# The two normalisations of the second norm stage: from VectorE to ScalarE, with a bias made by GpSimd

## The chip, the cores and the metric

The kernel runs on one core of one Trainium2 chip. The metric is the device time of one execution in microseconds (us), as the median of several runs. The engines of the core work side by side, each through its own list of instructions in order, and wait for one another on semaphores: TensorE (PE in the profile; its weight loads PEld), VectorE (DVE), ScalarE (ACT), GpSimd (POOL) and the DMA queues, of which SyncE (SP) issues most.

## The reference

The reference is two layers over 4096 tokens of 256 channels: `x = x + attention(norm(x)) + experts(norm(x))`, and then once more with other mixers. The part that matters here is where the second layer starts. It normalises each token, and one of its two mixers normalises the result again, with a weight and a bias of its own:

```
x  = x + L0_attn(xn, ...) + L0_ffn(xn, ...)
xn = _layernorm(x)                       # (x - m) / sqrt(v + eps)
x  = x + L1_attn(xn, ...) + L1_ffn(xn, ...)
# L1_ffn: mu, var of xn over the channels
#         z = (xn - mu) * rsqrt(var + EPS) * w + b, then q, k, v products of z
# L1_attn: q = elu(xn Wq + bq) + 1, k = elu(xn Wk + bk) + 1, v = xn Wv + bv, sums of k v
```

## The kernel before

The program is a row of phases with a barrier between them. The change lies in one, `phase_second_norm` (line 1382). It takes the 4096 tokens as 32 tiles of 128 tokens (on the partitions) by 256 channels, all in float32.

Each engine runs the same pipeline of steps (`steps`, line 1463). Step s works on four tiles at once: `a` is tile s, `b` tile s-1, `c` tile s-2 and `d` tile s-3. Four steps and the last five are written out, those between are a loop of two steps a pass. What each engine does in a step, in its own order, is the function `one` of its block:

- VectorE: `residual(a)` makes x1, the sum of the input, the attention result and two routed expert rows, and its statistics (L1716 to L1724); `sums(d)`; `keys_values(c)` (L1749 to L1753); `normed(a)` waits for the reciprocal root, makes xn1 (L1731, shown as `xn` in the profile) and the statistics of it (L1733, L1735); `queries(c)` (L1760, L1761, and L1763, which makes `k_feat`); `nested(a)` makes z (L1741); `values(c)` (L1769).
- GpSimd: `fetch(s + 1)`, two indirect DMAs that gather the routed rows of the next tile (L1531); `root(a, 0)`, which adds epsilon to the variance and raises it to -1/2 (L1540, L1542); `remainders(d)` (L1558, `qk_rest`); `root(a, 1)`, the same for the second norm; `add_base(a)` (L1547); `query_features(c)` (L1553).
- ScalarE: `key_exp(c)` (L1650); `low(d)` (L1681); `query_exp(c)` (L1654); `keep_turned(b)`, which takes the transposes of xn1 and z out of PSUM (L1660, and L1664 in two halves); `high(c)` (L1673, L1677).
- TensorE: `sums(d)` (L1627), which waits for `k_feat` of tile d; `linear(c)` (L1598, L1603); `nested_values(c)` (L1611); `turn(b)`, the transposes of xn1 and z (L1584, L1589); `nested_queries_keys(c)` (L1619).

So the order of each engine is written by hand, and `k_feat` of a step on VectorE (L1763), which stands behind the statistics of xn1, is what the next step on TensorE begins with.

Of the kernel before, what the change touches and what calls it, by code (L numbers as in the profile page):

```python
# [1381 lines left out]
def phase_second_norm(nc, g, ctx):  # L1382
# [4 lines left out]
    def sb(name, shape, dt=F32):  # L1387
        return ctx.enter_context(nc.sbuf_tensor(name, shape, dt))
# [13 lines left out]
    x1 = sb("x1", [P, 2, D])  # L1402
    stats = sb("s_stats", [P, 2, 2, 6])
    mean_var = sb("s_mean_var", [P, 2, 2, 2])
    var_eps = sb("s_var_eps", [P, 2, 2])
    rstd = sb("s_rstd", [P, 2, 2])
    xn1 = sb("xn1", [P, 2, D])
    base = sb("base", [P, 2, D])
    z = sb("z", [P, 2, D])
# [27 lines left out]
    cleared = sem("cleared")  # L1437
    x_d = [sem(f"x_in{r}") for r in range(2)]
    routed_in = [sem(f"routed_in{r}") for r in range(2)]
    half_d, routed_d, x1_d, st1_d, mv1_d, ve1_d, rs1_d, xn1_d, st2_d, mv2_d, ve2_d, rs2_d, z_d = (  # L1440
        sem(n) for n in ("half", "routed", "x1", "st1", "mv1", "ve1", "rs1", "xn1", "st2", "mv2", "ve2", "rs2", "z"))
    xnt_d, xns_d, zt_d, zs_d, kv_d, q_d, qk_d, v_d = (sem(n) for n in ("xnt", "xns", "zt", "zs", "kv", "q", "qk", "v"))
    kpre_d, vone_d, kmin_d, kexp_d, kf_d, sum_d, acc_d, qmin_d, qmax_d, qexp_d, qf_d = (
        sem(n) for n in ("kpre", "vone", "kmin", "kexp", "kf", "sum", "acc", "qmin", "qmax", "qexp", "qf"))
# [73 lines left out]
    @block.gpsimd  # L1518
    def _(pool):
        po = nc.gpsimd  # L1520
        po.memset(zeros[:], 0.0).then_inc(cleared, 1)
        po.memset(v_ones[:], 1.0).then_inc(cleared, 1)
        po.memset(g.v_one[:], 1.0).then_inc(cleared, 1)

        def fetch(t):

            r = t % 2
            if t >= 2:
                pool.wait_ge(x1_d, t - 1)
            for k in range(TOPK):  # L1530
                po.indirect_dma_start(share[:, r, k, :], None, g.y_d[:, :], bass.IndirectOffsetOnAxis(ap=g.slot[:, t, k:k + 1], axis=0)  # L1531
                                      ).then_inc(routed_in[r], 16)

        fetch(0)

        def root(a, n, mv_d, ve_d, rs_d, used_d):

            r = a.r
            wait_apart(pool, g, (used_d, a.free), (mv_d, a.t + 1))
            po.tensor_scalar(var_eps[:, r, n:n + 1], mean_var[:, r, n, 1:2], EPS, None, ALU.add).then_inc(ve_d, 1)  # L1540
            pool.wait_ge(ve_d, a.t + 1)
            po.tensor_tensor(rstd[:, r, n:n + 1], var_eps[:, r, n:n + 1], g.minus_half[:], ALU.pow).then_inc(rs_d, 1)  # L1542

        def add_base(a):
            pool.wait_ge(base_out[a.r], a.uses * 16)
            pool.wait_ge(xn1_d, a.t + 1)
            po.tensor_tensor(base[:, a.r, :], x1[:, a.r, :], xn1[:, a.r, :], ALU.add).then_inc(base_d, 1)  # L1547

        def query_features(c):
            pool.wait_ge(q_out[c.r], c.uses * 16)  # L1550
            pool.wait_ge(qmax_d, c.t * KC + KC)
            pool.wait_ge(qexp_d, c.t + 1)
            po.tensor_tensor(q_feat[:, c.r], q_max[:, c.r], q_min[:, c.r], ALU.add).then_inc(qf_d, 1)  # L1553

        def remainders(d):
            pool.wait_ge(lo_d, d.free)
            pool.wait_ge(hi_d, d.t + 1)
            po.tensor_tensor(qk_rest[:, d.r], qk_f[:, d.r], qk_parts[:, d.r, 0], ALU.subtract).then_inc(rest_d, 1)  # L1558

        for s in range(NT + 3):  # L1560
            a, c, d = (Tile(t, t % 2, t // 2) if 0 <= t < NT else None for t in (s, s - 2, s - 3))
            if s + 1 < NT:
                fetch(s + 1)
            if a is not None:
                root(a, 0, mv1_d, ve1_d, rs1_d, xn1_d)
            if d is not None:
                remainders(d)
            if a is not None:
                root(a, 1, mv2_d, ve2_d, rs2_d, z_d)
                add_base(a)  # L1570
            if c is not None:
                query_features(c)
# [71 lines left out]
    def _(act):  # L1644
        a_ = nc.scalar
# [6 lines left out]
        def query_exp(n):  # L1652
            act.wait_ge(qmin_d, n.t * KC + KC)
            a_.activation(q_min[:, n.r], q_min[:, n.r], ACT.Exp).then_inc(qexp_d, 1)  # L1654

        def keep_turned(b):
            t, r = b.t, b.r
            act.wait_ge(q_d, b.free)
            act.wait_ge(xnt_d, t + 1)
            a_.activation(xn1_t[:, r], p_xn[:, 0:D].rearrange("p (c t) -> p c t", c=KC), ACT.Copy).then_inc(xns_d, 1)  # L1660

            wait_apart(act, g, (qk_d, b.free), (zt_d, t + 1))
            for c in range(KC):
                last = a_.activation(z_t[:, r, c, :], p_z[:, c * P:(c + 1) * P], ACT.Identity,  # L1664
                                     bias=norm_t[:, 1, c, bass.ds(t, 1)], scale=norm_t[:, 0, c, bass.ds(t, 1)])
            last.then_inc(zs_d, 1)
# [12 lines left out]
        def low(d):  # L1679
            act.wait_ge(rest_d, d.t + 1)  # L1680
            a_.activation(qk_parts[:, d.r, 1], qk_rest[:, d.r], ACT.Copy).then_inc(lo_d, 1)  # L1681

        def one(ahead, a, b, c, d):
            if c is not None:
                key_exp(c)
            if d is not None:
                low(d)
            if c is not None:
                query_exp(c)
            if b is not None:  # L1690
                keep_turned(b)
            if c is not None:
                high(c)

# [3 lines left out]
    def _(dve):  # L1698
# [27 lines left out]
        def normed(a):  # L1726

            t, r = a.t, a.r
            dve.wait_ge(xnt_d, a.free)
            dve.wait_ge(rs1_d, t + 1)  # L1730
            v.tensor_scalar(xn1[:, r, :], x1[:, r, :], mean_var[:, r, 0, 0:1], rstd[:, r, 0:1], ALU.subtract, ALU.mult).then_inc(xn1_d, 1)  # L1731
            wait_apart(dve, g, (xn1_d, t + 1))
            v.bn_stats(stats[:, r, 1, :], xn1[:, r, :]).then_inc(st2_d, 1)  # L1733
            wait_apart(dve, g, (st2_d, t + 1))
            v.bn_aggr(mean_var[:, r, 1, :], stats[:, r, 1, :]).then_inc(mv2_d, 1)  # L1735

        def nested(a):
            t, r = a.t, a.r
            dve.wait_ge(zt_d, a.free)
            dve.wait_ge(rs2_d, t + 1)  # L1740
            v.tensor_scalar(z[:, r, :], xn1[:, r, :], mean_var[:, r, 1, 0:1], rstd[:, r, 1:2], ALU.subtract, ALU.mult).then_inc(z_d, 1)  # L1741

        def keys_values(n):

# [36 lines left out]
        def one(ahead, a, b, c, d):  # L1781
            if a is not None:
                residual(a)
            if d is not None:
                sums(d)
            if c is not None:
                keys_values(c)
            if a is not None:
                normed(a)
            if c is not None:  # L1790
                queries(c)
            if a is not None:
                nested(a)
            if c is not None:
                values(c)

        steps(dve, one)
# [585 lines left out]
```

## Time and profile before

| | us |
|---|---|
| median of 3 runs | 4898.24 (4896.6 to 4906.5) |
| the profiled execution: its time | 4895.71 |
| its span, first to last instruction | 4893.9 |
| its phase of the change: the first z tile starts at | 2634.4 |
| the last z tile starts at | 2891.0 |

The profile page gives busy time of the engines over the whole span (PE 92%, DVE 70%, ACT 39%, POOL 27%), which is a mean over phases with different limits. The phase of the change is some 270 us of the 4893.9, 5.5% of it. For what follows the span is cut: the list of instructions in order of time shows, for each, the start, the duration, the engine, the line of the kernel, and in brackets how long its engine had been idle before and what ended that. Times in the lists are counted from the start of the span.

### The profile page before, as it was taken

How to read it: one execution, taken by the hardware profiler on the slowest of the kernel's cores; microseconds unless marked ns; L12 is line 12 of the kernel's file. 1: busy time of each engine (PE TensorE's matmuls, PEld its weight loads, DVE VectorE, ACT ScalarE, POOL GpSimd, SP SyncE). 2: the span in 40 equal slices, each digit the busy share in tenths (PEclk: the TensorE clock that was granted, in tenths of full speed). 3: DMA queues.
4: the chain of work that ended last, by engine and by line, in shares of the span. 5: the costliest groups of instructions: out<-in, count | busy, mean ns of one | idle time of the engine just before them, and what ended most of it. 6: DMA issues, size and time to landing. Idle time of an engine off the chain costs nothing. (4 is left out here: it accounts for less than half of the span.)

```text
span 4893.9 us, 158526 instructions
## 1 busy us (share of the span) xinstructions
PE 4516.1 (92%) x65039; PEld 2896.2 (59%) x65039; DVE 3435.6 (70%) x5960; ACT 1910.9 (39%) x2645; POOL 1311.2 (27%) x1489
## 2 busy tenths in 40 slices
PE   6787859999999999999996879999999999999998
PEld 6333328999999999998664653444444444444443
DVE  4788975656565656555335978878787878787877
ACT  1566641111111111111143434656565656565654
POOL 1354444343434343433004772000000000000000
PEclk9999979999999999999998988999999999999999
DMA  3421231111111111110233441000000000000000
GB/s 109 139 98 56 103 130 52 55 55 55 53 56 53 56 52 58 47 63 26 74 121 105 109 118 35 4 17 4 17 4 17 4 17 6 17 9 13 9 13 9
DMA packets 201336, 249.92 MB, mean 51 GB/s; under 512 B 52864, under 2 KB 132864, under 8 KB 199968
## 3 DMA queue, kind: packets, MB, share of 16 engines
q1 hardware_dynamic: 180240, 209.39, 13.7%
q0 software_dynamic: 6144, 16.79, 1.1%
q10 hardware_dynamic: 14352, 14.55, 0.9%
q8 instruction: 522, 8.55, 0.7%
q14 instruction: 78, 0.64, 0.0%
HBM read 135.27 MB, written 105.38 MB: 49 GB/s over the span
## 5 line engine op out<-in xcount | busy, mean ns | idle before, releaser
L2169 DVE TENSOR_REDUCE part_max<-p_m 128x1 f32<-128x512 f32 x2118 | 1362.9, 685 | 377.7 <-PE p_m L2011 370.2
L2151 ACT ACTIVATE prob<-p_s 128x1024 f32<-128x1024 f32 x1024 | 1047.7, 1023 | 748.6 <-PE p_s L2075 746.5
L2030 PE MATMUL p_o<-prob,v_one 128*64 128x512 f32 x4096 | 1055.2, 592 | 3.9 <-ACT prob L2151 0.5
L2011 PE MATMUL p_m<-keys,queries 96*64 96x512 f16 x4236 | 661.9, 387 | 26.9 <-DMA keys<-parts_d 19.3
L2075 PE MATMUL p_s<-queries,keys 97*64 97x512 f16 x4096 | 619.6, 380 | 0.0
L2075 PEld LDWEIGHTS p_s<-queries,keys 97*64 97x64 f16 x4096 | 228.9, 109 | 597.7 <-issue 592.4
L1979 POOL TENSOR_TENSOR attn<-o_num,o_inv 32x512 f32<-32x512 f32 x64 | 81.0, 1266 | 1452.1 <-DVE o_inv L2188 1445.6
L546 PE MATMUL p_proj<-xn_t_all,proj_w_sb 128*128 (+1 forms) x768 | 390.0, 651 | 78.3 <-ACT raw L572 70.3
L2011 PEld LDWEIGHTS p_m<-keys,queries 96*64 96x64 f16 x4236 | 239.1, 108 | 309.1 <-DVE part_max L2169 56.3
L2030 PEld LDWEIGHTS p_o<-prob,v_one 128*64 128x64 f32 x4096 | 288.8, 136 | 162.1 <-issue 15.8
L805 PE MATMUL pd_pre<-inv,step 64*64 64x64 f32 x10240 | 372.0, 219 | 4.1 <-issue 2.7
L805 PEld LDWEIGHTS pd_pre<-inv,step 64*64 64x64 f32 x10240 | 339.5, 135 | 30.6 <-issue 29.7
L609 DVE SCALAR_TENSOR_TENSOR conv<-raw,conv_w_sb,conv 128x512 f32<-128x512 f32 x384 | 312.2, 813 | 56.8 <-POOL raw L633 45.3
L546 PEld LDWEIGHTS p_proj<-xn_t_all,proj_w_sb 128*128 128x128 f32 x768 | 155.6, 209 | 303.8 <-issue 178.3
L805 PE MATMUL pd_pre<-inv_low,upper 64*64 64x64 f32 x8192 | 302.4, 219 | 16.5 <-issue 15.5
L840 PE MATMUL pd_low<-step,inv 64*64 64x64 f32 x8192 | 297.7, 219 | 4.6 <-issue 3.8
L1040 DVE TENSOR_TENSOR step<-pd_pre,const 128x512 f32<-128x512 f32 x320 | 214.9, 687 | 118.4 <-PE pd_pre L805 116.5
L805 PEld LDWEIGHTS pd_pre<-inv_low,upper 64*64 64x64 f32 x8192 | 275.8, 135 | 24.8 <-issue 21.6
L840 PEld LDWEIGHTS pd_low<-step,inv 64*64 64x64 f32 x8192 | 274.1, 135 | 11.2 <-issue 10.3
L1044 DVE TENSOR_TENSOR inv_low<-low,pd_low 128x512 f32<-128x512 f32 x256 | 175.9, 687 | 125.1 <-PE pd_low L840 125.1
L1054 DVE TENSOR_TENSOR inv<-inv,pd_pre 128x512 f32<-128x512 f32 x256 | 175.9, 687 | 91.3 <-PE pd_pre L805 88.3
L1107 POOL TENSOR_TENSOR upper<-rel,beta 128x512 f32<-128x512 f32 x64 | 66.6, 1040 | 626.9 <-ACT rel L952 626.9
(246 smaller groups left out, 6832.7 us busy)
## 6 DMA issues: line engine op xcount, KB each, us to landing
k_d<-qkv SPq DMA_DIRECT2D x8, 2048.0 KB, 7.5
q_d<-qkv SPq DMA_DIRECT2D x8, 2048.0 KB, 12.3
v_d<-qkv SPq DMA_DIRECT2D x8, 2048.0 KB, 7.4
sums<-sums_d SPq DMA_DIRECT2D x128, 128.0 KB, 2.9
k_t<-k_d SPq DMA_DIRECT2D x64, 256.0 KB, 3.3
q_t<-q_d SPq DMA_DIRECT2D x64, 256.0 KB, 3.6
v_t<-v_d SPq DMA_DIRECT2D x64, 256.0 KB, 4.6
slots_d<-zero ACTq DMA_DIRECT2D x1, 10112.0 KB, 31.9
```

The source lines that it names most:

```text
L546: last = te.matmul(p_proj[j % RING][:], g.proj_w_sb[:, n, c, p * P:(p + 1) * P], g.xn_t[:, c, bass.ds(b * BLK, BLK)], start=c == 0, stop=c ...
L609: v.scalar_tensor_tensor(rows, cols, w, rows, ALU.mult, ALU.add).then_inc(conv_d, 1)
L805: last = te.matmul(out[hs, p, :], lhs(p, hs), rhs(p, hs), start=True, stop=True)
L840: last = te.matmul(p_low[x][hs, p, :], inv[x][hs, p, :], step[x][hs, p, :], start=k == 1 and p == 0, stop=k == NL - 1, skip_group_check=True)
L1040: v.tensor_tensor(step[x][:], p_pre[x][:], over_pairs(masks[:, k - 1, :]), ALU.mult).then_inc(step_d[x], 1)
L1044: v.tensor_tensor(inv_low[x][:], low_1[x][:], p_low[x][:], ALU.add).then_inc(lowc_d[x], 1)
L1054: v.tensor_tensor(inv[x][:] if k < NL else inv_fin[:, n.ring[x]], inv[x][:], p_pre[x][:], ALU.add).then_inc(up_d[x], 1)
L2011: last = te.matmul(p_m[k % 2][x * HALF:(x + 1) * HALF, :], queries[0:ROW, p, hh, at:at + HALF], keys[0:ROW, 2 * p + hh, kb * BLK:(kb + 1) ...
L2030: product = te.matmul(p_o[64 * hh:64 * hh + VW, :], g.v_one[:, j, p, hh:hh + 2, :].rearrange("p a d -> p (a d)"), prob[:, j % 2, hh, :], s ...
L2075: last = te.matmul(p_s[j % 2][x * HALF:(x + 1) * HALF, hh, :], keys[0:KR, 2 * p + hh, at:at + HALF], queries[0:KR, p, hh, :], start=True, ...
L2151: a.activation(prob[:, j % 2], p_s[j % 2][:], ACT.Exp, scale=SCORE_SCALE).then_inc(exp_d, 1)
L2169: v.tensor_reduce(part_max[:, hh * SUB + sub, kb:kb + 1], p_m[k % 2][:], AX.X, ALU.max).then_inc(red_d, 1)
```

## The change

The subtraction of the mean and the multiplication by the reciprocal root, `(x - m) * r`, becomes one ScalarE activation `x * r + (-m * r)`, with r as its scale and a new value, `shift` = -m * r, as its bias, both one number per partition. GpSimd makes `shift` behind each root, and waits for the root first. ScalarE gets `normed(a)` and `nested(a)`, and its order is changed: `keep_turned(b)`, which was fourth, is now first. VectorE keeps the statistics and waits for ScalarE where it waited for GpSimd.

```diff
         def root(a, n, mv_d, ve_d, rs_d, sh_d, used_d):
             r = a.r
             wait_apart(pool, g, (used_d, a.free), (mv_d, a.t + 1))
             po.tensor_scalar(var_eps[...], mean_var[:, r, n, 1:2], EPS, None, ALU.add).then_inc(ve_d, 1)
             pool.wait_ge(ve_d, a.t + 1)
             po.tensor_tensor(rstd[...], var_eps[...], g.minus_half[:], ALU.pow).then_inc(rs_d, 1)
+            pool.wait_ge(rs_d, a.t + 1)
+            po.tensor_scalar(shift[:, r, n:n + 1], mean_var[:, r, n, 0:1], rstd[:, r, n:n + 1], -1.0, ALU.mult, ALU.mult).then_inc(sh_d, 1)
...
     @block.scalar
+        def normed(a):
+            t, r = a.t, a.r
+            act.wait_ge(xnt_d, a.free)
+            act.wait_ge(base_d, a.free)
+            wait_apart(act, g, (sh1_d, t + 1))
+            a_.activation(xn1[:, r, :], x1[:, r, :], ACT.Identity, bias=shift[:, r, 0:1], scale=rstd[:, r, 0:1]).then_inc(xn1_d, 1)
+
+        def nested(a):
+            t, r = a.t, a.r
+            act.wait_ge(zt_d, a.free)
+            wait_apart(act, g, (sh2_d, t + 1))
+            a_.activation(z[:, r, :], xn1[:, r, :], ACT.Identity, bias=shift[:, r, 1:2], scale=rstd[:, r, 1:2]).then_inc(z_d, 1)
...
         def one(ahead, a, b, c, d):
+            if b is not None:
+                keep_turned(b)
+            if a is not None:
+                normed(a)
             if c is not None:
                 key_exp(c)
             if d is not None:
                 low(d)
+            if a is not None:
+                nested(a)
             if c is not None:
                 query_exp(c)
-            if b is not None:
-                keep_turned(b)
             if c is not None:
                 high(c)
...
     @block.vector
         def normed(a):
             t, r = a.t, a.r
-            dve.wait_ge(xnt_d, a.free)
-            dve.wait_ge(rs1_d, t + 1)
-            v.tensor_scalar(xn1[:, r, :], x1[:, r, :], mean_var[:, r, 0, 0:1], rstd[:, r, 0:1], ALU.subtract, ALU.mult).then_inc(xn1_d, 1)
             wait_apart(dve, g, (xn1_d, t + 1))
             v.bn_stats(stats[:, r, 1, :], xn1[:, r, :]).then_inc(st2_d, 1)
             wait_apart(dve, g, (st2_d, t + 1))
             v.bn_aggr(mean_var[:, r, 1, :], stats[:, r, 1, :]).then_inc(mv2_d, 1)
-
-        def nested(a):
-            t, r = a.t, a.r
-            dve.wait_ge(zt_d, a.free)
-            dve.wait_ge(rs2_d, t + 1)
-            v.tensor_scalar(z[:, r, :], xn1[:, r, :], mean_var[:, r, 1, 0:1], rstd[:, r, 1:2], ALU.subtract, ALU.mult).then_inc(z_d, 1)
```

One step of ScalarE behind the loop, before (`k_min` is L1650, `qk_rest` tile d, `ps_xn` and `ps_z` the transposes of tile b):

```order
L1650 ACTIVATE k_min<-k_min 128x256
L1681 ACTIVATE qk_parts<-qk_rest 128x512
L1654 ACTIVATE q_min<-q_min 128x256
L1660 ACTIVATE xn_t<-ps_xn 128x256
L1664 ACTIVATE z_t<-ps_z,norm_t 128x128 x2
L1673 ACTIVATE qk_f<-ps_qk,qk_b 128x128 x4
L1677 ACTIVATE qk_parts<-qk_f 128x512
```

The same step of ScalarE after:

```order
L1676 ACTIVATE xn_t<-ps_xn 128x256
L1680 ACTIVATE z_t<-ps_z,norm_t 128x128 x2
L1664 ACTIVATE xn<-x,s_shift,s_rstd 128x256
L1653 ACTIVATE k_min<-k_min 128x256
L1697 ACTIVATE qk_parts<-qk_rest 128x512
L1670 ACTIVATE z<-xn,s_shift,s_rstd 128x256
L1657 ACTIVATE q_min<-q_min 128x256
L1689 ACTIVATE qk_f<-ps_qk,qk_b 128x128 x4
L1693 ACTIVATE qk_parts<-qk_f 128x512
```

The new `xn` (L1664) stands behind the copies of both transposes, which come last but one in TensorE's step; `z` (L1670) stands ahead of the exponential of the queries.

One step of GpSimd, before, from the fetch on:

```order
L1531 DMA share_tile<-y_d,slot 128x256
L1531 DMA share_tile<-y_d,slot 128x256
L1540 TENSOR_SCALAR s_var_eps<-s_mean_var 128x1
L1542 TENSOR_TENSOR s_rstd<-s_var_eps,minus_half 128x1
L1558 TENSOR_TENSOR qk_rest<-qk_f,qk_parts 128x512
L1540 TENSOR_SCALAR s_var_eps<-s_mean_var 128x1
L1542 TENSOR_TENSOR s_rstd<-s_var_eps,minus_half 128x1
L1547 TENSOR_TENSOR base<-x,xn 128x256
L1553 TENSOR_TENSOR q_feat<-q_max,q_min 128x256
```

The same step of GpSimd after:

```order
L1532 DMA share_tile<-y_d,slot 128x256
L1532 DMA share_tile<-y_d,slot 128x256
L1541 TENSOR_SCALAR s_var_eps<-s_mean_var 128x1
L1543 TENSOR_TENSOR s_rstd<-s_var_eps,minus_half 128x1
L1545 TENSOR_SCALAR s_shift<-s_mean_var,s_rstd 128x1
L1561 TENSOR_TENSOR qk_rest<-qk_f,qk_parts 128x512
L1541 TENSOR_SCALAR s_var_eps<-s_mean_var 128x1
L1543 TENSOR_TENSOR s_rstd<-s_var_eps,minus_half 128x1
L1545 TENSOR_SCALAR s_shift<-s_mean_var,s_rstd 128x1
L1550 TENSOR_TENSOR base<-x,xn 128x256
L1556 TENSOR_TENSOR q_feat<-q_max,q_min 128x256
```

Two rows are new, one behind each root. VectorE's step loses L1731 and L1741 and is otherwise as before; TensorE's and SyncE's orders are unchanged.

## Rows read from the trace of the kernel before

**Rows 1.** Busy time by stretch: one step with 0.80 clock, one with 1.00, 28 steps together.
```profile
core 0: us, PE busy (x) PEld busy (x) DVE busy (x) ACT busy (x) POOL busy (x), PEclk, DMA share, GB/s
2673.16:2681.73 8.57, 8.07 (x41) 5.97 (x41) 7.59 (x20) 3.99 (x12) 6.42 (x10) 0.80 0.39 104
2681.73:2690.00 8.27, 6.38 (x41) 5.11 (x41) 7.57 (x20) 4.09 (x12) 6.44 (x10) 1.00 0.43 116
2656.56:2891.18 234.62, 198.92 (x1121) 152.46 (x1121) 212.64 (x533) 113.62 (x309) 178.58 (x251) 0.91 0.40 108
```

**Rows 2.** TensorE's wait in those 28 steps: us in total, times, longest.
```profile
PE ps_sum L1627 <- DVE k_feat L1763: 35.9, 29, 1.9
```

**Rows 3.** TensorE in order of time, two steps: start us, us, engine, line.
```profile
2664.89 0.68 PE L1627 MATMUL ps_sum<-v_ones,k_feat 128*128 128x129 f32 x4 [1.95 <-DVE k_feat L1763]
...
2669.10 0.38 PE L1589 MATMUL ps_z<-const,z 128*128 128x128 f32 x2
...
2673.16 1.09 PE L1627 MATMUL ps_sum<-v_ones,k_feat 128*128 128x129 f32 x4 [1.89 <-DVE k_feat L1763]
2674.04 3.20 PE L1598 MATMUL ps_kv<-kv_w,xn_t 128*128 128x512 f32 x4
...
2679.06 0.38 PE L1589 MATMUL ps_z<-const,z 128*128 128x128 f32 x2
```

**Rows 4.** All engines in order of time, the end of the second of these steps.
```profile
2673.57 0.77 POOL L1553 TENSOR_TENSOR q_feat<-q_max,q_min 128x256 f32<-128x256 f32 x1
...
2676.88 0.24 POOL L1540 TENSOR_SCALAR s_var_eps<-s_mean_var 128x1 f32<-128x1 f32 x1
...
2677.76 1.15 POOL L1558 TENSOR_TENSOR qk_rest<-qk_f,qk_parts 128x512 f32<-128x512 f32 x1
...
2678.06 1.01 DVE L1753 TENSOR_SCALAR k_min<-k_pre 128x256 f32<-128x256 f32 x1
...
2678.98 0.40 DVE L1731 TENSOR_SCALAR xn<-x,s_mean_var,s_rstd 128x256 f32<-128x256 f32 x1
...
2679.49 0.43 DVE L1733 BATCH_NORM_STATS2 s_stats<-xn 128x6 f32<-128x256 f32 x1
...
2680.39 0.22 POOL L1540 TENSOR_SCALAR s_var_eps<-s_mean_var 128x1 f32<-128x1 f32 x1 [1.48 <-DVE s_mean_var L1735]
...
2680.70 0.57 POOL L1542 TENSOR_TENSOR s_rstd<-s_var_eps,minus_half 128x1 f32<-128x1 f32 x1
...
2681.03 0.42 ACT L1654 ACTIVATE q_min<-q_min 128x256 f32<-128x256 f32 x1 [0.99 <-DVE q_min L1760]
...
2681.23 0.94 POOL L1547 TENSOR_TENSOR base<-x,xn 128x256 f32<-128x256 f32 x1
...
2681.50 0.83 DVE L1741 TENSOR_SCALAR z<-xn,s_mean_var,s_rstd 128x256 f32<-128x256 f32 x1
2681.61 0.80 ACT L1664 ACTIVATE z_t<-ps_z,norm_t 128x128 f32<-128x128 f32 x2
...
2681.73 0.68 PE L1627 MATMUL ps_sum<-v_ones,k_feat 128*128 128x129 f32 x4 [0.50 <-DVE k_feat L1763]
...
2682.30 0.63 ACT L1673 ACTIVATE qk_f<-ps_qk,qk_b 128x128 f32<-128x128 f32 x2
```

**Rows 5.** Groups by line over those 28 steps: count, busy us, mean ns, idle.
```profile
L1731 DVE TENSOR_SCALAR xn<-x,s_mean_var,s_rstd 128x256 f32<-128x256 f32 x28 | 26.9, 961 | 0.1
```

**Rows 6.** Groups by line and shape, ScalarE and GpSimd, whole span.
```profile
L1664 ACT ACTIVATE z_t<-ps_z,norm_t 128x128 f32<-128x128 f32 x64 | 25.6, 454 | 2.3 <-PE ps_z L1589 2.3
L1328 ACT ACTIVATE e_act_h<-e_bank 128x128 f32<-128x128 f32 x79 | 21.9, 277 | 65.0 <-PE e_bank L1288 65.0
L1961 POOL TENSOR_SCALAR nest_ob<-nest_o,const 128x32 f32<-128x32 f32 x4 | 1.4, 352 | 0.0
```

**Rows 7.** In order of time, the first tile: z's transpose and ScalarE's copy.
```profile
2635.32 0.66 PE L1589 MATMUL ps_z<-const,z 128*128 128x128 f32 x2 [2.06 <-DVE z L1741]
...
2636.10 0.81 ACT L1664 ACTIVATE z_t<-ps_z,norm_t 128x128 f32<-128x128 f32 x2 [2.35 <-PE ps_z L1589]
```

More of the change, by code:

```diff
@@ L1406, in phase_second_norm @@
     rstd = sb("s_rstd", [P, 2, 2])
+    shift = sb("s_shift", [P, 2, 2])
     xn1 = sb("xn1", [P, 2, D])
@@ L1439, in phase_second_norm @@
     routed_in = [sem(f"routed_in{r}") for r in range(2)]
-    half_d, routed_d, x1_d, st1_d, mv1_d, ve1_d, rs1_d, xn1_d, st2_d, mv2_d, ve2_d, rs2_d, z_d = (
-        sem(n) for n in ("half", "routed", "x1", "st1", "mv1", "ve1", "rs1", "xn1", "st2", "mv2", "ve2", "rs2", "z"))
+    half_d, routed_d, x1_d, st1_d, mv1_d, ve1_d, rs1_d, sh1_d, xn1_d, st2_d, mv2_d, ve2_d, rs2_d, sh2_d, z_d = (
+        sem(n) for n in ("half", "routed", "x1", "st1", "mv1", "ve1", "rs1", "sh1", "xn1", "st2", "mv2", "ve2", "rs2", "sh2", "z"))
     xnt_d, xns_d, zt_d, zs_d, kv_d, q_d, qk_d, v_d = (sem(n) for n in ("xnt", "xns", "zt", "zs", "kv", "q", "qk", "v"))
@@ L1534, in _, with root @@
         fetch(0)
-        def root(a, n, mv_d, ve_d, rs_d, used_d):
+        def root(a, n, mv_d, ve_d, rs_d, sh_d, used_d):
             r = a.r
@@ L1564, in _ @@
             if a is not None:
-                root(a, 0, mv1_d, ve1_d, rs1_d, xn1_d)
+                root(a, 0, mv1_d, ve1_d, rs1_d, sh1_d, xn1_d)
             if d is not None:
@@ L1568, in _ @@
             if a is not None:
-                root(a, 1, mv2_d, ve2_d, rs2_d, z_d)
+                root(a, 1, mv2_d, ve2_d, rs2_d, sh2_d, z_d)
                 add_base(a)
@@ L1791, in one @@
                 queries(c)
-            if a is not None:
-                nested(a)
-            if c is not None:
                 values(c)
```

## The prediction

> **What bounds the stage now.** I read the busy time by stretch first. From 2656.56 to 2891.18 us, 28 steps take 234.62 us, 8.38 each. TensorE is busy for 198.92 of them, VectorE for 212.64, GpSimd for 178.58, ScalarE for 113.62 [rows 1]. VectorE is the fullest engine. The waits say the same: TensorE waits 35.9 us in 29 pieces for VectorE's `k_feat` [rows 2], and the list in order of time shows GpSimd idle for 1.48 us before the second root [rows 4], while VectorE's group of xn has 0.1 us of idle before it in 28 steps [rows 5]. So a step lasts as long as VectorE's list of work.
>
> The list in order of time then shows two things that the sums hide.
>
> First, one VectorE instruction in each step is long. With `qk_rest` running on GpSimd from 2677.76 for 1.15 us, `k_min` takes 1.01 us and xn behind it 0.40; where `qk_rest` meets xn, xn is the long one, and its mean is 961 ns [rows 4, 5].
>
> Second, TensorE's clock. After an idle of 1.89 us before `ps_sum` (TensorE then waits for `k_feat`) the granted clock falls to its 1.2 GHz level: the step from 2673.16 has 0.80 on the mean, the next 1.00, and from `ps_sum` to the transpose of z it takes 5.90 us (2673.16 to 2679.06) where it took 4.21 (2664.89 to 2669.10), 1.69 more [rows 1, 3]. Of the 28 steps, 15 begin with an idle of 1.87 us or more, and in 12 of these `ps_kv` takes 2.84 us or more, as the 3.20 in [rows 3]; the other 13 begin with 0.51 us or less, as the 0.50 in [rows 4], and all 13 run at the full clock. Today this hardly costs: the step with the low clock lasts 8.57 us against 8.27 [rows 1], 0.30 of the 1.69. VectorE has other work meanwhile, and TensorE catches up by a short idle in the next step.
>
> **What is removed.** Per step, VectorE loses xn (0.96 mean) and z (0.83) [rows 4, 5]: 1.79 of its 7.6 busy us. If VectorE's list still set the step, that would be the gain.
>
> **What is added.** On ScalarE two activations of 128x256 with scale and bias per partition. No row has that form from SBUF. The exponential of the same size takes 0.42 [rows 4]; 128x128 takes 454 ns with both operands per partition and 277 with neither [rows 6], 0.18 more. I take 0.42 + 0.18 = 0.60; the bounds are 0.42 (operands free) and 0.80 (as the pair of `z_t`) [rows 4]. On GpSimd two instructions `shift` of one element. The nearest rows are `var_eps` at 0.22 [rows 4] and a `tensor_scalar` of 32 elements at 352 ns [rows 6]; I take 0.25. Each waits for its root, as the root waits for `var_eps`: 2680.39 + 0.22 to 2680.70, a gap of 0.09. So from root to the next instruction it takes 0.57 + 0.09 + 0.25 = 0.91 where it took 0.53 (2680.70 to 2681.23) [rows 4], 0.38 more, twice a step. GpSimd's idle hides that, if nothing waits for the root; now two things do.
>
> **What is moved, and closes a loop.** `keep_turned(b)` is now first on ScalarE, and xn of tile a stands behind it. So xn waits for TensorE's transposes, and these stand behind `ps_sum`, `ps_kv`, `ps_q`, `ps_v` of the same step. VectorE's statistics wait for xn, `queries` and `k_feat` stand behind the statistics, and the next step's `ps_sum` waits for `k_feat`. That is a ring, once round per step, in which nothing can run ahead. Before, xn waited for a root alone. I walk the ring with starts from [rows 3, 4, 7]:
>
> - statistics of xn to `ps_sum`: 2679.49 to 2681.73, 2.24;
> - `ps_sum` to the transpose of z: 4.21 at the full clock;
> - that transpose, 0.38 long, and the hop to ScalarE (2635.32 + 0.66 to 2636.10, 0.12): 0.50;
> - two copies `z_t` to the next ScalarE instruction: 2681.61 to 2682.30, 0.69;
> - xn 0.60 and the hop to the statistics (2678.98 + 0.40 to 2679.49, 0.11): 0.71.
>
> Sum 8.35 us at the full clock. In a step with the low clock all of the 1.69 lies on the ring: 10.04.
>
> A second ring runs through GpSimd, since ScalarE's `q_min` now stands behind z, and z behind `shift`: statistics to `var_eps` 0.90; to the root 0.31; to `shift` 0.66; `shift` and hop 0.37; z to the next activation 0.49 (0.60 less the overlap of 0.11 that the pair of `z_t` shows); exponential 0.42 and hop 0.11; that is 3.26 for `q_feat`. Then `q_feat` to the next step's `var_eps` 3.31 (2673.57 to 2676.88, with the two fetches between); root 0.31, `shift` 0.66, 0.37; xn and hop 0.71. Sum 8.62 [rows 4]. This sets the steps at the full clock. `base` is not late in it: 2.12 + 0.91 = 3.03 is before 3.26.
>
> Queued behind the waiting xn on ScalarE are `k_min`, `qk_parts` and z; they are awaited by `k_feat`, 1.68 us or more after the statistics, which leaves them time. The DMA of SyncE that follows `qk_parts` is not in a ring.
>
> **How often the clock falls.** After `ps_z` TensorE has `ps_qk` left. Round the first ring the idle before `ps_sum` is what it was in the steps that ended at 1.9, in every step, since TensorE no longer catches up: 0.50 is gone from the list. At the share of the trace, 12 of 15, that is 22 of 28 steps.
>
> The sum: 22 steps x (10.04 - 8.38) = 36.5; 6 x (8.62 - 8.38) = 1.4; for the filling and the end of the pipeline, where `shift` and a longer activation stand in the chain of each tile, 2, an estimate. Together +40 us. The profiled execution takes 4895.7 (span 4893.9), so 4936; the median shown is 2.5 above it: 4938. With activations of 0.42 it is 22 x 1.48 - 6 x 0.12 + 2 = +34, with 0.80 it is 22 x 1.86 + 6 x 0.64 + 2 = +47: 4932 to 4945.
>
> A rule on the clock, from the Trainium skill, "TensorE: Matmul & The Clock Gate", section "HAM oscillation — how this bites in real kernels", says that a loop which does a short burst of matmuls and then waits goes back to the half clock in every round. By the rule all 28 steps pay: 28 x 1.66 + 2 = +48, 4946; by the trace, 3 of 15 such idles were followed by no fall (one of them is the 1.95 before 2664.89 in [rows 3]), and the sum above goes by these.
>
> **Rivals.**
>
> *Faster: VectorE is relieved, and GpSimd becomes the bound.* For it: VectorE's and not TensorE's list is full, and the long xn goes. GpSimd would need 8.57 - 1.48 = 7.09 us and two times 0.38 more, 7.85: 28 x (7.85 - 8.38) = -15, 4883. It needs a first ring below 7.85, 0.50 less than the walk gives, and the low clock off it; if xn did not have to wait for the transposes it would be so. Against it stands the order of ScalarE, which puts them first. The skill's page "SBUF — State Buffer", section "Who interferes with whom", speaks for this rival: a VectorE `tensor_scalar` in its two-port mode and a GpSimd instruction lock each other out for the whole instruction, so taking two of them away frees both engines. The trace agrees on the cause (1.01 or 0.40 us for the same work, [rows 4]); but what it frees is time outside both rings.
>
> *Little change: the low clock stays hidden or grows rare.* If the falls hit `ps_qk`, which is in no ring, or came as seldom as one step in ten, the steps are at 8.62: 28 x 0.24 + 2 = +9, 4907. Against it: the falls came at once after the idle, in `ps_sum` or `ps_kv`, which are in the ring.
>
> *Half of the steps*, as 12 of 28 now: 14 x 1.66 + 14 x 0.24 + 2 = +29, 4927. For it: the fall has not come in two steps in a row in this trace. Against it: each was followed by a step with an idle of 0.51 or less, which the ring no longer gives.
>
> That the change does not do what it says can be left out: the order shows both activations and both shifts in each step.
>
> **Chances and range.** The forecast of +34 to +48 has 0.60, half of the steps 0.17, little change 0.10, faster 0.05, and 0.08 for more (hops of ScalarE longer than those of VectorE in both rings, 0.2 in each of 28 steps, 6 us more). The time is 4938. The range is 4905 to 4952; the likeliest case alone has 4928 to 4950. About 0.2% (9.8 us) is what a measurement of this kernel can tell from no change; the case of little change lies on that line. So slower 0.86, the same 0.09, faster 0.05.
>
> **What would show it.** In the profile after: steps of 10.0 us and of 8.6, no longer 8.57 and 8.27; VectorE idle before the statistics of xn (some 1.5 us at the full clock, 3 at the low one), released by ScalarE's xn; ScalarE's xn released by TensorE's `ps_z` in the steps with the low clock and by `shift` in the others; an idle of 1.9 to 2.1 us before every `ps_sum`, and no 0.5; a granted clock of 0.86 or so over the stage where it was 0.91; `k_min` still at 0.3 or 1.0. The prediction is wrong if the steps at the low clock are not longer by 1.4 or more, if they are less than half, or if xn starts before the transposes of its step.

## The result, and the profile after

The kernel after takes 4951.77 us (median of 4 runs, 4949.41 to 4954.13), the kernel before on the same chip 4901.93 (4 runs, 4896.6 to 4906.5). The ratio is 1.0102, with a 95% interval of 1.0085 to 1.012: slower by 49.8 us. Forecast were 4938, a range of 4905 to 4952, and slower with 0.86. The direction came out. The time lies at the upper edge of the range, 0.2 us inside it, and above the 4928 to 4950 of the likeliest case.

The profiled execution takes 4953.73 us (span 4951.9) where it took 4895.7 (span 4893.9). From the first z to the last z it is 305.7 us (2639.84 to 2945.56) against 256.5, so 49.2 of the 58.0 us of difference lie in the tile pipeline; 5.4 come up to the first z (4.0 of these ahead of the stage, in a part that the change does not touch) and 3.4 behind the last one, also untouched.

Busy time by stretch, kernel after: the stretch in us, its length, busy us (instructions) of the five engines, granted clock, DMA share, GB/s. A step at the low clock (one in which the granted clock falls to 1.2 GHz for a part of it), one at the full clock, and 28 steps together, against [rows 1].

```profile
core 0: us, PE busy (x) PEld busy (x) DVE busy (x) ACT busy (x) POOL busy (x), PEclk, DMA share, GB/s
2756.59:2766.75 10.16, 8.06 (x41) 6.02 (x41) 6.37 (x18) 5.06 (x13) 7.02 (x12) 0.83 0.34 92
2797.19:2806.21 9.02, 6.38 (x41) 5.11 (x41) 6.11 (x18) 5.28 (x13) 7.01 (x12) 1.00 0.35 96
2654.97:2937.10 282.13, 222.42 (x1120) 163.67 (x1121) 175.77 (x477) 141.87 (x364) 196.67 (x309) 0.84 0.34 90
```

A step lasts 10.08 us where it lasted 8.38. No engine is fuller than TensorE, with 7.9 of the 10.08 us, and part of that is the low clock's own doing. VectorE has fallen from 7.6 busy us per step to 6.3, as was wanted; GpSimd has 7.0. When no list of work fills a step, the order in which the engines wait for each other sets it.

Waits over these 28 steps, kernel after (who waits, for whom: us in total, times, longest), against [rows 2].

```profile
ACT xn_t L1676 <- PE ps_xn L1587: 90.9, 28, 3.4
DVE s_stats L1750 <- ACT xn L1664: 83.1, 28, 3.4
PE ps_sum L1630 <- DVE k_feat L1774: 62.2, 28, 4.5
POOL s_var_eps L1541 <- DVE s_mean_var L1752: 46.1, 28, 2.0
ACT z L1670 <- POOL s_shift L1545: 45.5, 28, 2.1
POOL q_feat L1556 <- ACT q_min L1657: 13.8, 28, 0.5
```

Read in a circle: ScalarE waits for TensorE's transposes, VectorE for ScalarE's xn, TensorE for VectorE's `k_feat`, each 28 times in 28 steps. Before, the third had 35.9 us [rows 2], and VectorE did not wait for xn at all [rows 5]. The last three rows are the second circle, through GpSimd.

The first circle in order of time, kernel after, one step at the low clock (start us, duration, engine, line, instruction; in brackets the idle before it and its releaser), against [rows 3, 4].

```profile
2754.35 0.43 DVE L1750 BATCH_NORM_STATS2 s_stats<-xn 128x6 f32<-128x256 f32 x1 [3.15 <-ACT xn L1664]
...
2756.59 0.68 PE L1630 MATMUL ps_sum<-v_ones,k_feat 128*128 128x129 f32 x4 [2.10 <-DVE k_feat L1774]
...
2757.11 2.99 PE L1601 MATMUL ps_kv<-kv_w,xn_t 128*128 128x512 f32 x4
...
2762.47 0.38 PE L1592 MATMUL ps_z<-const,z 128*128 128x128 f32 x2
...
2762.74 0.38 ACT L1676 ACTIVATE xn_t<-ps_xn 128x256 f32<-128x256 f32 x1 [3.39 <-PE ps_xn L1587]
...
2763.11 0.81 ACT L1680 ACTIVATE z_t<-ps_z,norm_t 128x128 f32<-128x128 f32 x2
...
2763.81 0.59 ACT L1664 ACTIVATE xn<-x,s_shift,s_rstd 128x256 f32<-128x256 f32 x1
...
2764.51 0.43 DVE L1750 BATCH_NORM_STATS2 s_stats<-xn 128x6 f32<-128x256 f32 x1 [3.15 <-ACT xn L1664]
```

From statistics to statistics it is 10.16 us, the length of the step: 2.24 to `ps_sum`, 5.88 to the transpose of z, 0.64 to `z_t`, 0.70 to xn, 0.70 to the statistics. In before the stretch from `ps_sum` to that transpose was as long at the low clock (5.90, [rows 3]), but in no circle that set the step.

The second circle in the same view, kernel after, at the full clock, against [rows 4].

```profile
2798.36 0.99 POOL L1556 TENSOR_TENSOR q_feat<-q_max,q_min 128x256 f32<-128x256 f32 x1 [0.51 <-ACT q_min L1657]
...
2801.91 0.23 POOL L1541 TENSOR_SCALAR s_var_eps<-s_mean_var 128x1 f32<-128x1 f32 x1
...
2803.27 0.60 ACT L1664 ACTIVATE xn<-x,s_shift,s_rstd 128x256 f32<-128x256 f32 x1 [0.42 <-POOL s_shift L1545]
...
2803.97 0.43 DVE L1750 BATCH_NORM_STATS2 s_stats<-xn 128x6 f32<-128x256 f32 x1 [2.31 <-ACT xn L1664]
...
2805.85 0.34 POOL L1545 TENSOR_SCALAR s_shift<-s_mean_var,s_rstd 128x1 f32<-128x1 f32 x1
...
2806.31 0.60 ACT L1670 ACTIVATE z<-xn,s_shift,s_rstd 128x256 f32<-128x256 f32 x1 [1.37 <-POOL s_shift L1545]
...
2807.39 0.99 POOL L1556 TENSOR_TENSOR q_feat<-q_max,q_min 128x256 f32<-128x256 f32 x1 [0.51 <-ACT q_min L1657]
```

Here `shift` and not the transposes releases xn, and from `q_feat` to `q_feat` it is 9.03 us. Of the 28 steps 26 are at the low clock with 10.04 to 10.19 us, 10.16 on the mean, and two at the full clock with 9.02 and 9.03. The sum is 26 x (10.16 - 8.38) + 2 x (9.02 - 8.38) = 47.6, which leaves 1.6 of the 49.2 for both ends of the pipeline.

### The profile page after: what moved, and what is told of

Same layout as the page of the kernel before. It is cut to its first block and busy times, and to the rows that moved or that the text cites. A ratio compares the mean times of both kernels' runs of the same rounds, so it can differ in the third digit from the quotient of the medians.

```text
span 4951.9 us, 158647 instructions
## 1 busy us (share of the span) xinstructions
PE 4544.3 (92%) x65039; PEld 2905.6 (59%) x65039; DVE 3394.5 (69%) x5896; ACT 1943.2 (39%) x2709; POOL 1328.7 (27%) x1553
```

## The experiments

They ran on three chips, on which the kernel before takes 4885.65 to 4892.08 us (medians), so each kernel is compared by its ratio to before on its own chip; the ratios are estimated from all runs and differ by up to 0.0006 from the quotient of the two medians. "Ring" in what follows is a circle of waits as above: ring 1 goes through TensorE, ring 2 through GpSimd. Four questions: are the two rings real and do they have these sizes (1, 2, 7)? Is it the order on ScalarE by itself (3, 6)? What is the relief of VectorE worth once no ring through TensorE takes it (4, 5)? What takes it then (8 to 10)?

### 1. xn ahead of the kept transposes

```diff
         def one(ahead, a, b, c, d):
-            if b is not None:
-                keep_turned(b)
             if a is not None:
                 normed(a)
+            if b is not None:
+                keep_turned(b)
```

> The changed kernel with one swap on ScalarE: normed(a) ahead of keep_turned(b); all else as changed. Theory (the ring through TensorE's transposes): xn waits for its shift alone, TensorE and its low clock leave the ring, every step lasts what the ring through GpSimd lasts, 9.02 us in the changed kernel's steps at the full clock: 28 x (9.02 - 10.08) = -30, so about 4922 against 4952. The low clock may still be seen, but costs under 0.5 us a step. Rival (the two activations and the two shifts cost it, wherever they stand): 4945 to 4955, steps stay at 10.1.

Measured: 4902.68 against 4885.65, ratio 1.0041 (1.0026 to 1.0057). Busy time by stretch: one step at the full clock, one at the low clock, then 27 together.

```profile
2747.32:2756.34 9.02, 6.38 (x40) 5.11 (x40) 6.12 (x19) 4.95 (x14) 7.02 (x12) 1.00 0.38 102
2793.19:2802.20 9.01, 8.07 (x40) 5.96 (x41) 6.24 (x18) 4.95 (x13) 7.22 (x13) 0.81 0.40 102
2648.98:2892.51 243.53, 188.38 (x1081) 146.32 (x1081) 169.16 (x460) 133.77 (x351) 189.54 (x298) 0.93 0.38 102
```

ScalarE in order of time, same kernel.

```profile
2763.22 0.60 ACT L1664 ACTIVATE xn<-x,s_shift,s_rstd 128x256 f32<-128x256 f32 x1 [3.32 <-POOL s_shift L1545]
2763.73 0.36 ACT L1676 ACTIVATE xn_t<-ps_xn 128x256 f32<-128x256 f32 x1
```

Here xn is released by `shift`, no longer by a transpose. (In 5 of 24 waits the profile names `ps_xn`; it ends then at the same time as `shift`, and it belongs to a later tile than the one that xn has to wait for.) The 27 steps have 9.02 on the mean, most of them 9.01 or 9.02, one 8.75 and three 9.12 to 9.16. The clock still falls in 10 of the 27 (in after in 26 of 28), and these ten have 9.06 on the mean, so that the low clock now costs next to nothing. 0.0061 of the 0.0102 go with two calls that change places, and no instruction more or less. Ring 1 is thus shown; what is left, 9.02 a step, is ring 2. The idle before `ps_sum` is 2.4 to 2.6 us in 17 of these steps and no longer than 1.3 in the others; the clock falls after 10 of the 17. So the length of the idle alone does not say whether it falls.

### 2. Fourteen matmuls more in each step, to hold the clock

```diff
             if c is not None:
                 nested_queries_keys(c)
+                for _ in range(14):
+                    te.matmul(p_fill[:, 0:P], g.c("eye"), g.c("eye"), start=True, stop=True)
```

> The changed kernel with 14 matmuls of 128x128 (identity times identity into a spare PSUM bank, read by nobody) behind nested_queries_keys of each step, so that TensorE's 2.1 us of idle before ps_sum is nearly full. Theory (it is the low clock that lengthens the ring through TensorE, 1.7 us in a step): the granted clock stays at 1.00, 25 of 28 steps fall from 10.16 to 9.02, -28 us, about 4924. Rival (the low clock is a mark of waiting and not its cause): steps stay at 10.1, 4952 or more. If the fill itself runs into the next step at the low clock, above 4960.

Measured: 4920.2 against 4885.65, ratio 1.007 (1.0055 to 1.0085). Busy time of 29 steps together.

```profile
2654.93:2923.86 268.93, 268.93 (x1975) 236.83 (x1973) 178.72 (x486) 147.88 (x382) 197.26 (x311) 1.00 0.36 97
```

TensorE in order of time, same kernel: the filling, and the `ps_sum` behind it.

```profile
2744.54 3.29 PE L1644 MATMUL ps_fill<-const 128*128 128x128 f32 x28
2747.66 0.50 PE L1630 MATMUL ps_sum<-v_ones,k_feat 128*128 128x129 f32 x3
```

The clock is 1.00 throughout and a step 9.27 us, 0.8 less than in after, although TensorE computes more. But TensorE is never idle (busy for 268.93 of 268.93 us): the filling is longer than the wait that it was to fill, and TensorE's own list sets the step. The cost of the clock is shown, the size of ring 2 is not. Experiment 7 mends that.

### 3. Before, with only ScalarE's order changed

```diff
         def one(ahead, a, b, c, d):
+            if b is not None:
+                keep_turned(b)
             if c is not None:
                 key_exp(c)
...
-            if b is not None:
-                keep_turned(b)
```

> The kernel before with the new order of ScalarE alone: keep_turned(b) first, both normalisations on VectorE, no shift. Theory (a ring needs xn behind the transposes): xn does not wait for ScalarE, the loop from ps_sum over the copies to key_exp, k_feat and the next ps_sum is 4.85 + 0.70 + 0.41 + 0.7 = 6.7 us, 8.4 at the low clock, which just about fits under the 8.38 of a step: 4900 to 4912. Rival (the order alone brings the loss, since ScalarE stands still before the transposes): 4940 to 4955.

Measured: 4886.02 against 4885.65, ratio 1.0003 (0.9993 to 1.0012): no difference. Steps of 8.37; busy time over 232.00 us.

```profile
2656.00:2888.00 232.00, 195.22 (x1114) 149.88 (x1112) 210.41 (x529) 111.12 (x302) 176.38 (x249) 0.92 0.40 108
```

Waits, same kernel.

```profile
ACT xn_t L1660 <- PE ps_xn L1584: 90.8, 26, 4.6
```

ScalarE stands still for the transposes as long as in after (90.9 us there), and it costs nothing, since nothing behind it on ScalarE feeds the statistics. What does stand behind it, the exponential for `k_feat`, closes a shorter ring, put at 6.7 us (8.4 at the low clock) in the expectation, which fits under the step. Neither the order nor the long wait is slow by itself; xn behind it makes the ring.

### 4. Only z on ScalarE, xn back on VectorE

```diff
+            v.tensor_scalar(xn1[:, r, :], x1[:, r, :], mean_var[:, r, 0, 0:1], rstd[:, r, 0:1], ALU.subtract, ALU.mult).then_inc(xn1_d, 1)
...
+            if n == 1:
+                po.tensor_scalar(shift[:, r, n:n + 1], mean_var[:, r, n, 0:1], rstd[:, r, n:n + 1], -1.0, ALU.mult, ALU.mult).then_inc(sh_d, 1)
...
-ScalarE: keep_turned(b) normed(a) key_exp(c) low(d) nested(a) query_exp(c) high(c)
+ScalarE: key_exp(c) low(d) query_exp(c) keep_turned(b) nested(a) high(c)
```

The last two lines of this diff sum up ScalarE's order and are not code.

> Half of the change: z on ScalarE behind the copies of the transposes (order key_exp, low, query_exp, keep_turned, nested, high), one shift on GpSimd for it, xn on VectorE as before. Theory: no ring through ScalarE; VectorE's list is 0.75 us shorter and GpSimd's 0.38 longer (7.09 + 0.38 = 7.5), steps of 7.6 to 7.8, 28 x 0.7 = -20, about 4883: faster than both kernels. Rival (VectorE's list was not the bound, or GpSimd's fetch and roots are): 4895 to 4905.

Measured: 4893.66 against 4885.65, ratio 1.0021 (1.001 to 1.0031); steps of 8.63. This missed: less than 8 was expected. All engines in order of time.

```profile
2734.51 1.15 POOL L1562 TENSOR_TENSOR qk_rest<-qk_f,qk_parts 128x512 f32<-128x512 f32 x1
2734.63 1.18 DVE L1750 TENSOR_SCALAR xn<-x,s_mean_var,s_rstd 128x256 f32<-128x256 f32 x1 [0.17 <-POOL s_rstd L1543]
...
2735.92 0.43 DVE L1752 BATCH_NORM_STATS2 s_stats<-xn 128x6 f32<-128x256 f32 x1
...
2736.82 0.23 POOL L1541 TENSOR_SCALAR s_var_eps<-s_mean_var 128x1 f32<-128x1 f32 x1 [1.15 <-DVE s_mean_var L1754]
```

Walked from here there is a ring of GpSimd's roots: statistics to `var_eps` 0.90, root 0.30, `shift` 0.68, `base` 0.30, `q_feat` 0.69, the fetches 1.07 + 1.37 + 1.04, root 0.31, to xn 0.68, to the statistics 1.29; 8.63 together. The same walk in before gives 8.33 with the 1.25 that xn takes where it meets `qk_rest`, beside the 8.38 of VectorE's list. So the kernel before had two limits of nearly one length, and taking one away could bring an estimated 0.05 us a step. In this ring xn meets `qk_rest` in nearly every step and takes about 1.18.

### 5. The fetches behind the first root

```diff
-            if s + 1 < NT:
-                fetch(s + 1)
             if a is not None:
                 root(a, 0, mv1_d, ve1_d, rs1_d, sh1_d, xn1_d)
+            if s + 1 < NT:
+                fetch(s + 1)
```

on top of experiment 4.

> The half change of e4 (z alone on ScalarE) with GpSimd's fetch(s + 1) moved from ahead of root(a, 0) to behind it. In e4 the steps were 8.63, and the walk finds a ring through GpSimd: statistics of xn, second root, shift, base, q_feat, two fetches, first root, xn. Theory (rings set the step, and the fetches are 2.4 us of this one): with the fetches behind the root nothing awaited stands behind them, and the step falls to VectorE's or GpSimd's list, 7.6 to 7.9: 28 x (7.7 - 8.38) = -19, some 4883 where before is 4902, ratio 0.996. Rival (the lists' own length, with the longer residual of VectorE, sets it): 8.3 or more, ratio 1.000. A third way: the gathered rows land too late for residual (2.8 us from issue), steps of 8.0 to 8.4.

Measured: 4882.29 against 4886.87, ratio 0.9993 (0.9984 to 1.0002): the best of all versions, and not told apart from before. Busy time, one step.

```profile
2665.03:2673.21 8.18, 6.65 (x41) 5.18 (x41) 7.48 (x19) 4.48 (x13) 6.98 (x10) 1.00 0.42 112
```

The ring no longer sets the step: VectorE waits for another engine for 4.0 us in 26 steps, so its own list does. And yet the step falls only to 8.18 (the clock falls in 4 of 26 steps, in before in 12 of 28). VectorE is at 7.48 busy us in this step, 7.33 on the mean. Its group of `k_feat` (count, busy us, mean ns, idle), and the same place in order of time.

```profile
L1776 DVE SCALAR_TENSOR_TENSOR k_feat<-k_pre,k_min 128x256 f32<-128x256 f32 x26 | 39.2, 1507 | 0.0
```

```profile
2736.97 1.66 DVE L1776 SCALAR_TENSOR_TENSOR k_feat<-k_pre,k_min 128x256 f32<-128x256 f32 x1
2737.17 1.17 POOL L1562 TENSOR_TENSOR qk_rest<-qk_f,qk_parts 128x512 f32<-128x512 f32 x1
```

`k_feat` now meets `qk_rest` in each step and takes 1.51 us on the mean where it took 0.41 in before; xn, which no longer meets it, fell to 0.42. Against the 0.83 of z and the 0.54 of xn that VectorE was spared, `k_feat` takes 1.10 more and the residual's last two instructions 0.20 more each (0.68 against 0.48).

### 6. Experiment 1, and the exponential of the queries ahead of z

```diff
-            if a is not None:
-                nested(a)
             if c is not None:
                 query_exp(c)
+            if a is not None:
+                nested(a)
```

> e1 (both normalisations on ScalarE, xn ahead of the copies) with query_exp ahead of nested. Theory (the 9.01 of e1 is the ring through GpSimd with z and q_min's exponential in it, 3.41 us to q_feat): q_feat then waits for base alone, 0.90 + 0.31 + 0.67 + 0.30 + 0.72 = 2.9, so steps of 8.5 to 8.6, 28 x 0.45 = -13 us against e1, ratio to before 1.001. Rival (e1's 9.01 is GpSimd's list, or ScalarE): no change against e1, ratio 1.004.

Measured: 4889.46 against 4886.87, ratio 1.0006 (0.9997 to 1.0015). Busy time over 210.14 us of its steps.

```profile
2661.63:2871.77 210.14, 178.06 (x1000) 136.68 (x1001) 154.89 (x426) 126.17 (x325) 172.57 (x276) 0.91 0.41 109
```

With both calls moved, the whole change, its two activations and two shifts included, costs nothing that can be measured (8.41 a step on the mean, most 8.38 or 8.39; somewhat more was expected). Ring 2 is thus shown from its other side: what it had above this was the wait of the exponential behind z. VectorE has 6.2 busy us in these 8.4, 1.4 less than before, and nobody gains by it.

### 7. Ten matmuls in place of fourteen

```diff
-                for _ in range(14):
+                for _ in range(10):
```

> e2 with 10 matmuls in place of 14. In e2 TensorE had no idle at all and its own list with the fill, 9.27, set the step. Theory: 10 of them (0.207 each by e2) leave 0.5 us of idle and the clock at 1.00, the ring through GpSimd sets the step, 9.02, 28 x 0.25 = -7 us against e2, ratio to before 1.0055. Rival (the low clock comes back as soon as there is idle): steps of 10.1, ratio 1.010.

Measured: 4904.18 against 4886.87, ratio 1.0039 (1.0024 to 1.0053). Busy time of 26 steps, 9.01 each on the mean.

```profile
2655.72:2890.03 234.31, 223.99 (x1560) 190.97 (x1561) 162.97 (x443) 137.30 (x338) 182.09 (x287) 1.00 0.38 102
```

TensorE in order of time, same kernel.

```profile
2736.68 0.35 PE L1630 MATMUL ps_sum<-v_ones,k_feat 128*128 128x129 f32 x1 [0.40 <-DVE k_feat L1776]
```

TensorE again waits a little for `k_feat`, so its list is not the limit; the clock stays at 1.00, and the step is 9.02, as in experiment 1 by the other way. With the order of after untouched, the clock alone makes 10.16 of 9.02.

### 8. Experiment 5 without `shift`

```diff
-            pool.wait_ge(rs_d, a.t + 1)
-            po.tensor_scalar(shift[:, r, n:n + 1], mean_var[:, r, n, 0:1], rstd[:, r, n:n + 1], -1.0, ALU.mult, ALU.mult).then_inc(sh_d, 1)
...
-            a_.activation(z[:, r, :], xn1[:, r, :], ACT.Identity, bias=shift[:, r, 1:2], scale=rstd[:, r, 1:2]).then_inc(z_d, 1)
+            a_.activation(z[:, r, :], xn1[:, r, :], ACT.Copy, scale=rstd[:, r, 1:2]).then_inc(z_d, 1)
```

It leaves out the subtraction of the mean of xn.

> e5 with the shift left out: xn1 is already normalised, so its mean is zero but for rounding, and z is computed as xn1 times its reciprocal root, a ScalarE copy with a scale per partition. The subtraction of that mean is what the kernel leaves out. In e5 a step of 8.18 had GpSimd idle for 0.42 only (awaiting the first statistics), and VectorE's k_feat held up behind qk_rest (0.9 to 1.7 for 0.41 us). Theory (the shift costs GpSimd's list 0.67 per step, and that list still sets the step): 7.6 to 7.8, 28 x 0.45 = -13 us against e5, ratio to before 0.996 to 0.997. Rival (VectorE's list with its held-up instructions sets it): 8.1 to 8.2, ratio 0.999. Rival two (the step follows from how k_feat and qk_rest meet): anywhere between, with k_feat at 0.41.

Measured: 4896.78 against 4892.08, ratio 1.001 (1.0001 to 1.0019), steps of 8.46: longer than in experiment 5, with one instruction less. The group of the residual's instruction (same columns as above), and a wait.

```profile
L1736 DVE SCALAR_TENSOR_TENSOR x<-share_tile,weight,x 128x256 f32<-128x256 f32 x49 | 40.2, 820 | 7.1
```

```profile
POOL s_var_eps L1541 <- DVE s_mean_var L1740: 32.1, 25, 1.3
```

GpSimd waits 1.3 us in each step for VectorE, so its list is not the limit (in experiment 5 it had 0.4). `k_feat` has 1.39 and the residual 0.82 each, where before had 0.41 and 0.48. VectorE waits little (0.26 us a step for `k_pre`, 0.15 in experiment 5), so its list sets the step as in experiment 5, and it is fuller: 7.50 busy us a step against 7.33. The two differences, 0.17 and 0.11, make up the 0.28 by which the step is longer. That its instructions are longer because both engines meet at other places fits this, and no run separates it.

### 9. Experiment 5, the remainders last on GpSimd

```diff
-            if d is not None:
-                remainders(d)
             if a is not None:
                 root(a, 1, mv2_d, ve2_d, rs2_d, sh2_d, z_d)
                 add_base(a)
             if c is not None:
                 query_features(c)
+            if d is not None:
+                remainders(d)
```

and `low(d)` last on ScalarE.

> e5 with GpSimd's qk_rest moved from between the roots to the end of its step (and ScalarE's low(d), which needs it, to the end of ScalarE's). In e5, k_feat on VectorE took 0.9 to 1.7 us where qk_rest ran beside it. Theory (VectorE's list is as long as the GpSimd work that meets its instructions with two SBUF operands; in e5 that list sets the step): k_feat back at 0.41, the pair of residual no longer than 1.5, steps of 7.6 to 8.0, ratio to before 0.996 to 0.998. Rival (GpSimd's own list sets it): steps 8.1 to 8.2, ratio 0.999. If qk_rest then meets residual, k_pre or k_min instead, 8.2 to 8.5.

Measured: 4901.02 against 4888.66, ratio 1.0023 (1.0014 to 1.0031), steps of 8.67: missed, 7.6 to 8.0 was expected. The residual's group, and the place in order of time.

```profile
L1739 DVE SCALAR_TENSOR_TENSOR x<-share_tile,weight,x 128x256 f32<-128x256 f32 x48 | 46.7, 973 | 34.8 <-DMA share_tile<-y_d,slot 31.3
```

```profile
2734.82 2.05 DVE L1739 SCALAR_TENSOR_TENSOR x<-share_tile,weight,x 128x256 f32<-128x256 f32 x2 [1.35 <-DMA share_tile<-y_d,slot]
...
2735.25 1.34 POOL L1562 TENSOR_TENSOR qk_rest<-qk_f,qk_parts 128x512 f32<-128x512 f32 x1
...
2737.87 0.22 POOL L1541 TENSOR_SCALAR s_var_eps<-s_mean_var 128x1 f32<-128x1 f32 x1 [1.28 <-DVE s_mean_var L1743]
...
2740.28 0.97 POOL L1532 DMA_INDIRECT share_tile<-y_d,slot  x1 [0.30 <-DVE s_mean_var L1754]
...
2743.40 2.12 DVE L1739 SCALAR_TENSOR_TENSOR x<-share_tile,weight,x 128x256 f32<-128x256 f32 x2 [1.27 <-DMA share_tile<-y_d,slot]
```

`k_feat` is back at 0.41, but the meeting only moved: the residual's two instructions, 0.48 each in before, now take 0.97 each beside `qk_rest`. And they wait 1.35 us for the gathered rows, which the later fetch brings later; that wait is new.

These two are links of one new ring, in which both engines wait in each of 24 steps (31.3 us for the gather on VectorE, 30.8 for `s_mean_var` L1743 on GpSimd): from the residual to its statistics 2.15, to `var_eps` 0.90, to the root 0.31, to the first fetch 0.74, to the second 1.36, and from there to the next residual 3.12; 8.58 in this step, 8.67 on the mean.

### 10. Experiment 9 without `shift`

The edits of 8 and 9 together; it leaves out the subtraction of the mean of xn.

> e9 without the shift, that is without subtracting the mean of xn1 in z, which is zero but for rounding. e8, without the shift, was slower than e5 (8.45 against 8.18 a step), with the pair of residual at 1.78 in place of 1.50. Theory (where GpSimd's work meets VectorE's decides, the length of GpSimd's list does not): the sign of e10 against e9 is open, but the step follows the sum of k_feat and residual. Rival (GpSimd's list): 0.67 shorter than e9 in each step, -19 us.

Measured: 4893.57 against 4888.66, ratio 1.0009 (0.9999 to 1.0019), steps of 8.50, `k_feat` 0.41, the residual 0.90 each. It is 0.17 a step below experiment 9 and not the 0.67 of the rival (GpSimd's list); the residual's pair is 0.15 shorter. The ring of experiment 9 is there too (VectorE waits 31.9 us in 25 steps for the gather, GpSimd 39.0 for `s_mean_var`). So what sets the step is VectorE's list in 5 and 8, and the ring through the gather, with the stretched residual in it, in 9 and 10. No version beats before by more than the measurement can tell.

## Why the prediction was right, and where its sizes were off

**The reading of before.** That VectorE's list was a limit is right, that it was the only one is not. Experiment 4 found the ring of GpSimd's roots, 8.33 in before against 8.38. The forecast does not hang on it, but the rival "faster" does: it priced the new bound by GpSimd's list, 7.85, where a ring had to be priced (8.63 in experiment 4). Even without ring 1 and the clock, its 15 us were not there; experiment 6, its best case, gives 1.0006.

**What is removed.** VectorE's 1.8 us a step lie outside what sets the step, as stated. They did not go in full (7.6 to 6.3 busy): of the residual's three instructions the first grew from 0.61 to 0.83 and the other two from 0.48 to 0.62 each, beside a GpSimd that is busier, while `k_min` fell from 0.54 to 0.33 and takes 1.0 nowhere. The prediction had no term for that.

**The activations.** 594 and 600 ns measured, 0.60 taken, out of bounds of 0.42 to 0.80. The Trainium skill, "ScalarE: Activation LUTs", section "What ACT_TABLE_LOAD costs", gives a cost by elements and by operands per partition that comes to an estimated 585 ns for this form; the trace agrees.

**Ring 1.** Forecast 10.04, measured 10.16 (and shown as a ring by experiments 1 and 7). The stretches of 2.24, 0.69 and 0.71 came out as 2.24, 0.70 and 0.70; `ps_sum` to `ps_z` was 5.90 and is 5.88. The step that was short is "that transpose and the hop to ScalarE, 0.50": `z_t` does not stand behind the transpose alone, but also behind `xn_t`, which starts at 2762.74 and lasts 0.38; it is 0.64. The instruction ahead on the same engine was forgotten. Over 26 steps the ring's 0.12 is 3 us.

**Ring 2.** Forecast 8.62, measured 9.02. Of the 0.40, 0.24 are in "`q_feat` to the next step's `var_eps`", 3.55 where 3.31 was read off before: `q_feat` takes 0.99 in place of 0.77, with the residual on VectorE beside it (2798.28 for 1.35 us). 0.06 are in `q_feat` behind z, 0.10 in `shift` and z behind the statistics (the second `shift` takes 0.34, not 0.25). It counts in two steps only, 0.8 us.

**How often the clock falls.** Taken 22 of 28, measured 26. This is the term with the largest error, 4 x (10.04 - 8.62) = 5.7 us; it was scaled from 12 of 15 idles in a kernel where each fall was followed by a step with nearly no idle. That share does not carry over: it is 26 of 28 in after and 10 of 17 in experiment 1, with idles that are no shorter, and what decides it stays open. So that the term came within 4 steps of 26 is in part luck. Beside it I had put a rule of the Trainium skill, "TensorE: Matmul & The Clock Gate", section "HAM oscillation — how this bites in real kernels": such a loop goes back to the half clock in every round. The loop of that section waits longer than it computes, so it says less of this case than I let it say; the trace of after comes near the rule, with two exceptions in 28, and its 4946 was nearer than my 4938, while experiment 1 goes against it.

**The marks.** A clock of 0.86 was 0.84. VectorE's idle of 3 us at the low clock was 3.15, but at the full one 2.31 and not 1.5. The releaser of xn changes with the clock as stated. "Longer by 1.4 or more" at the low clock holds against the 8.57 of before (10.16, 1.59 more), but not against the full-clock steps of after (9.02, 1.14 more), since ring 2 is 0.40 longer than forecast: the low clock costs what ring 1 exceeds ring 2 by, and the two were taken 1.42 apart.

**The sum.** 26 x 1.78 + 2 x 0.64 + 1.6 = 49.2 against 36.5 + 1.4 + 2 = 40. The 9.2 missing are 5.7 from the count, 3.1 from ring 1, 0.8 from ring 2, less 0.4 at the ends. The three errors of size point the same way. The median is 49.8 above that of before, outside the +34 to +48 that had 0.60; of the 13.8 us between 4938 and 4951.77, 3.7 are only that before's own median came out at 4901.93 and not at 4898.24. The mechanism and the direction were right; that the time is still in the range is owed to its width, with 0.2 us to spare. Of the rivals, "half of the steps" and "little change" fell with the count of low steps, and no condition of theirs was met.

## What to carry to other kernels

When work moves to an engine with time to spare, ask first behind what it stands there, and walk from its result back to itself through every engine: if the way closes within one round, the length of that way is the step, whatever the busy times say. One swap of two calls on ScalarE was worth 30 us here, and the relief of VectorE nothing, since a second limit of nearly the same length lay beside the first. And keep TensorE out of such a ring: with a wait of 2 us in each round its clock fell in 26 of 28 steps, which costs little as long as TensorE can catch up (experiment 1), and is paid as far as its ring exceeds the next one once it cannot (10.16 against 9.02).

## What the runs showed of the hardware

- With `qk_rest` on GpSimd beside it, a VectorE `scalar_tensor_tensor` with two operands from SBUF takes 1.66 us where it takes 0.41 alone, a `tensor_scalar` from SBUF 1.18 against 0.40. In the orders tried here the meeting moved from xn and `k_min` to `k_feat` and to the residual, and did not go away.
- A wait of 2.1 us of TensorE in each step, with 8.06 us of matmuls around it, goes with a fall of the granted clock in 26 of 28 steps; ten matmuls of 128x128 in the wait hold it at 1.00, with 0.41 us of idle left. An idle is no sure sign of a fall: in experiment 1 idles of 2.4 to 2.6 us are followed by one in 10 of 17 steps. For fourteen of them the row in experiment 2 has 3.29 us (recorded as x28), 0.24 each.
- A GpSimd instruction of one element takes 0.22 to 0.34 us, and the next that needs its result starts 0.08 to 0.10 later (2804.87 + 0.23 to 2805.18, 2805.18 + 0.57 to 2805.85). In the step of the second circle a root and its `shift` take 0.89 and 0.98 up to the next instruction, where a root alone has 0.53 [rows 4].
